# A Macaron block on one core: Y of the next batch made earlier, W of the last two batches on two engines, a clearing moved

## Chip, cores and metric

The kernel runs on 1 core of one Trainium2 chip. The metric is the device time of one execution in microseconds (us), lower is better. The core has five engines that run side by side and meet at semaphores: TensorE (PE), VectorE (DVE), ScalarE (ACT), GpSimd (POOL) and SyncE (SP, which issues DMAs here).

## The reference, cut to what matters

The block is FFN, attention, FFN over x of shape (8, 512, 256) in float32, each with a layer norm ahead and a residual behind. The FFNs have a shared expert and 8 routed ones, one per token. The diff's main part is in the attention:

```
k, q, v = split_heads(x @ Wk), split_heads(x @ Wq) / 4, split_heads(x @ Wv)   # 16 heads of 16
q_l, k_l = means over 8 neighbours -> 64 landmarks per head
s1 = softmax(q @ k_l.T)      # 512 x 64
s2 = softmax(q_l @ k_l.T)    # 64 x 64
s3 = softmax(q_l @ k.T)      # 64 x 512
z = s2.T / (max column sum * max row sum)
for _ in range(6):
    xz = s2 @ z
    z = 0.25 * z @ (13 I - xz @ (15 I - xz @ (7 I - xz)))
out = s1 @ (z @ (s3 @ v))    # then out @ Wo + bo
```

## The kernel before

The program has three parts: the first FFN (`ffn_*(0)`), the attention (`attention_*`) and the second FFN (`ffn_*(1)`). Each engine has its own hand-written list of instructions. An engine works through its list in order; a wait holds everything behind it on that engine.

**Attention.** The 8 batches (512 tokens, `GW`) go through a pipeline by periods, `for b in PERIODS` (-3 to 7). In period `b` the iterations for the inverse of batch `b` run, as the one serial chain, and all other work is put between its steps: for `nxt = b + 1` the maxima and exponentials of s3, s2 and s1, `T = s3 v`, and the start of its chain; for `far = b + 2` the transposes and projections to q and k; for `old = b - 1` the sums over heads and the denominators; for `done = b - 2` the output projection.

The inverse is not formed. The chain keeps, for each of 8 head pairs, X = [Y | T-part], 64 + 16 columns (`XC`, one buffer for even and one for odd batches). Y starts as s2.T s2, scaled (`start_y`: 32 small products on TensorE, L1909, into two of the banks 2 to 5; the scaling on DVE, L865). T's part starts as a product with s2 (`start_t`, L1954, copied by ACT, L1234, `product_kept`). One iteration `it` (0 to 5) is:

- POOL makes W = Y - I, in two halves of 4 pairs (`chain_w`, L1490); there is one buffer W;
- TensorE's **first product** W X (`chain_first`, L1933);
- ACT makes BU from it (`chain_b`, L1197), DVE makes ST (`chain_s`, L885), each in two halves, where the first half of the one is ahead of the second half of the other;
- TensorE's **second product** (`chain_second`, L1946);
- DVE updates X in two halves (`chain_x`, L896).

Around it, by name and line: `s3_max` (TensorE L1840, DVE L798, 4 reads of 128x1024) and `s1_max` (L1875 and L805, 4 reads, "quarters") make the products whose row maxima DVE takes; all of them, `s2_scores` (L1848), the exponentials' products, Y's products and the spread denominators (L1975) share banks 2 to 5 (`grid`). `landmarks` (L778) sums q and k, `query_block` (L783) lays q_l out by blocks; ACT rounds that to `QBDR` (L1315). `turn_nm1` (L1857) transposes the maxima of s1, ACT keeps them (L1312). `heads` (L1961), `denominators` (L1967, reciprocal on DVE L905), `heads_norm` (DVE L911) serve batch `old`. `project_qk` (L1823), four groups of 6 matmuls per batch, and `column_sums` (L1913; its maximum is DVE's `column_max`, L842, then `pair_scale`, L849) share bank 6; the row sums go `turn_rows`, `row_max`, `spread_rows` (L1903), `row_kept` (L837). `project` (L1580) is the output projection, `project_v` (L1833) that of v. `low_outputs` (POOL L1512) makes the low parts that `project` needs.

At the end of period `b` before the change, DVE took all four quarters of the s1 maxima before T's scaling, X's last update and Y's scaling; TensorE waited for these maxima before Y's products; POOL made the first W after Y's scaling, and the next first product waited for that W.

**Routed tiles.** In the FFN the tokens are gathered in 39 tiles (13 x 3). TensorE multiplies a tile with the expert's gate and up weights (`through`, L1735), each split in a high part (ACT L1115) and a low part (DVE L679, `low_weights`). `RY` holds three tiles of results; DVE clears it once (L703), and POOL's first gathers of residuals into it wait for that (`ry_clear`).

## Time and profile before

| what | value |
|---|---|
| median of 3 runs (lowest, highest) | 1156.12 us (1154.26, 1157.37) |
| the profiled execution's own time | 1155.66 us |
| its span | 1153.8 us |
| mean granted TensorE clock | 0.979 |
| busy: PE, DVE, ACT, POOL | 94%, 66%, 51%, 49% |
| share of the chain that ended last: PE, DVE, ACT | 83%, 9%, 3% |

Read it so: the span is the profiled part of one execution, and 1.9 us of its time lie around it. Busy shares are of the whole span; the attention lies between about 400 and 778 us of it. The chain that ended last is the row of work that set the end, followed back from the last instruction. A granted clock of 1.00 is 2.4 GHz, 0.50 is 1.2 GHz.

### The profile page before, as it was taken

How to read it: one execution, taken by the hardware profiler on the slowest of the kernel's cores; microseconds unless marked ns; L12 is line 12 of the kernel's file. 1: busy time of each engine (PE TensorE's matmuls, PEld its weight loads, DVE VectorE, ACT ScalarE, POOL GpSimd, SP SyncE). 2: the span in 40 equal slices, each digit the busy share in tenths (PEclk: the TensorE clock that was granted, in tenths of full speed). 3: DMA queues.
4: the chain of work that ended last, by engine and by line, in shares of the span. 5: the costliest groups of instructions: out<-in, count | busy, mean ns of one | idle time of the engine just before them, and what ended most of it. 6: DMA issues, size and time to landing. Idle time of an engine off the chain costs nothing.

```text
span 1153.8 us, 30074 instructions
## 1 busy us (share of the span) xinstructions
PE 1088.2 (94%) x11278; PEld 878.9 (76%) x11279; DVE 758.1 (66%) x1401; ACT 584.3 (51%) x961; POOL 565.5 (49%) x774
## 2 busy tenths in 40 slices
PE   8999999999999678899999998779999999999997
PEld 6788888888888557677667677558888888888886
DVE  6736746676767557778878867655346566767674
ACT  4334336666665445465465564344443256566663
POOL 5720734667675624345435442336301726666664
PEclk9999999999999887999999999889999999999999
DMA  7272144222211210000000000004241242212220
GB/s 255 74 306 96 37 147 143 61 73 68 68 60 38 92 56 2 3 3 3 3 3 3 3 3 3 20 21 182 92 183 37 73 161 69 64 62 61 73 64 14
DMA packets 39472, 80.25 MB, mean 70 GB/s; under 512 B 6452, under 2 KB 31159, under 8 KB 38336
## 3 DMA queue, kind: packets, MB, share of 16 engines
q1 hardware_dynamic: 27568, 52.94, 12.8%
q0 software_dynamic: 11232, 25.20, 7.1%
q8 instruction: 81, 1.33, 0.5%
q10 hardware_dynamic: 560, 0.52, 0.1%
q14 instruction: 31, 0.25, 0.1%
HBM read 57.13 MB, written 27.00 MB: 73 GB/s over the span
## 4 chain that ended last, share of the span: by engine, by line
PE 83%; DVE 9%; ACT 3%; issue 2%; POOL 2%; DMA 1%; ACTq 0%; DVEq 0%; POOLq 0%
PE PS L1735 19%; PE PS L1649 12%; PE PS L1749 12%; PE PS L1665 7%; PE PS L1823 3%; DVE A_NM L805 3%; PE PS L1742 3%; PE PS L1933 3%; PE PS L1946 2%; PE PS L1833 2%; PE PS L1580 2%; PE PS L1683 2%; PE PS L1961 1%; PE PS L1893 1%; PE PS L1867 1%
## 5 line engine op out<-in xcount | busy, mean ns | idle before, releaser
L1735 PE MATMUL PS<-WHL,XGH 128*128 128x512 f32 x624 | 217.4, 429 | 2.1 <-DVE WHL L679 2.1
L1749 PE MATMUL PS<-WD,XNT 128*128 x624 | 149.7, 383 | 1.5 <-ACT XNT L1129 1.5
L1490 POOL TENSOR_TENSOR A_W<-A_XC,CB 128x256 f32<-128x256 f32 x96 | 69.8, 748 | 153.0 <-DVE A_XC L896 131.4
L700 DVE SCALAR_TENSOR_TENSOR XNT<-PS,SCORES,XNT 128x512 f32<-128x512 f32 x78 | 58.6, 751 | 120.5 <-PE PS L1735 109.9
L1398 POOL DMA_INDIRECT X<-xs_dram,WHO x78 | 103.2, 1323 | 57.6 <-issue 23.1
L1124 ACT ACTIVATE XNT<-PS,SCORES 128x512 f32<-128x512 f32 x78 | 53.8, 689 | 145.7 <-PE PS L1735 143.7
L1735 PEld LDWEIGHTS PS<-WHL,XGH 128*128 128x128 f32 x624 | 111.4, 189 | 20.4 <-DVE WHL L679 2.6
L1749 PEld LDWEIGHTS PS<-WD,XNT 128*128 128x128 f32 x624 | 112.6, 190 | 16.0 <-issue 2.2
L1735 PE MATMUL PS<-WHL,XGL 128*128 128x512 f32 x312 | 123.2, 395 | 0.0
L1392 POOL TENSOR_SCALAR XNT<-WD 128x128 f32<-128x128 f32 x64 | 52.5, 840 | 128.7 <-DVE WD L573 128.7
L1665 PE MATMUL PS<-SDH,HHL 128*128 128x256 f32 x512 | 103.9, 287 | 1.7 <-DVE X L613 1.3
L630 DVE TENSOR_TENSOR HHL<-HSB,HHL 128x512 fp32r<-128x512 f32 x64 | 45.8, 715 | 82.0 <-ACT HHL L1089 82.0
L1404 POOL DMA_INDIRECT HSB<-shared_dram,WHO x78 | 80.5, 1032 | 38.7 <-issue 18.9
L679 DVE TENSOR_TENSOR WHL<-WG,WHL 128x1024 fp32r<-128x1024 f32 x78 | 94.8, 1216 | 3.3 <-ACT WHL L1115 3.3
L1089 ACT CAST HHL<-HSB 128x512 fp32r<-128x512 f32 x64 | 39.7, 620 | 112.7 <-PE PS L1665 76.1
L679 DVE TENSOR_TENSOR WHL<-WU,WHL 128x1024 fp32r<-128x1024 f32 x78 | 95.5, 1224 | 0.0
L1665 PEld LDWEIGHTS PS<-SDH,HHL 128*128 128x128 f32 x512 | 82.8, 188 | 10.4 <-issue 9.2
L1115 ACT CAST WHL<-WG 128x1024 fp32r x78 | 82.5, 1058 | 1.7 <-issue 1.7
L1115 ACT CAST WHL<-WU 128x1024 fp32r x78 | 82.5, 1057 | 0.0
L1649 PE MATMUL PS<-XHL,SGH 128*128 128x512 f32 x256 | 80.8, 397 | 1.5 <-DVE XHL L460 1.5
L1649 PE MATMUL PS<-XHL,SUH 128*128 128x512 f32 x256 | 81.1, 399 | 0.0
L1083 ACT ACTIVATE HSB<-PS 128x512 f32<-128x512 f32 x64 | 38.3, 599 | 79.1 <-PE PS L1649 78.9
(273 smaller groups left out, 2527.0 us busy)
## 6 DMA issues: line engine op xcount, KB each, us to landing
xs_dram<-WG SPq DMA_DIRECT2D x16, 512.0 KB, 3.0
WU<-in_r_up SPq DMA_DIRECT2D x2, 4096.0 KB, 15.1
shared_dram<-X SPq DMA_DIRECT2D x16, 512.0 KB, 2.9
WG<-in_r_gate SPq DMA_DIRECT2D x2, 4096.0 KB, 17.1
WD<-in_r_down SPq DMA_DIRECT2D x4, 2048.0 KB
X<-in_x SPq DMA_DIRECT2D x7, 512.0 KB, 9.1
X<-mid_dram SPq DMA_DIRECT2D x7, 512.0 KB, 3.9
X<-xs_dram,WHO POOLq DMA_INDIRECT x78
```

The lines of the kernel that those rows point to most:

```text
L679: dve.tensor_tensor(WHL[2 * slot + 1][:], B[w][:, bass.ds(ex * (KD * F), KD * F)], WHL[2 * slot][:].bitcast(F32), ALU.subtract).then_inc(s ...
L700: dve.scalar_tensor_tensor(B["RH"][:, u * F:(u + 1) * F], banks[3 + u][:], score(t), B["RS"][:, u * F:(u + 1) * F], ALU.mult, ALU.mult).th ...
L1115: act.copy(WHL[2 * slot][:], B[w][:, bass.ds(ex * (KD * F), KD * F)]).then_inc(s["whi"], 1)
L1124: act.activation(B["RS"][:, u * F:(u + 1) * F], banks[1 + u % 2][:], ACT.Silu, scale=B["SCORES"][:, bass.ds(t, 1)]).then_inc(s["rsilu"], 1)
L1392: hot = pool.tensor_scalar(B["ROW_HOT"][t], B["ROW_NO"], B["SROWF"][:, t:t + 1], None, ALU.is_equal)
L1398: pool.indirect_dma_start(out=B["XS"][:, u * D:(u + 1) * D], out_offset=None, in_=xs_dram, in_offset=bass.IndirectOffsetOnAxis(ap=B["WHO"] ...
L1404: pool.indirect_dma_start(out=B["RY"][:, u * D:(u + 1) * D], out_offset=None, in_=shared_dram, in_offset=bass.IndirectOffsetOnAxis(ap=B["W ...
L1490: pool.tensor_tensor(B["W"][:].rearrange("p (a m) -> p a m", m=M)[:, part, :], B["XC"][b % 2][:].rearrange("p (a w) -> p a w", w=XW)[:, pa ...
L1649: ins = pe.matmul(banks[bank][:], w[:, part], tok[:, k * GW:(k + 1) * GW], start=at == 0, stop=at == len(steps) - 1)
L1665: ins = pe.matmul(to, h[:, j * P:(j + 1) * P], w[:, part], start=(f == 0 and i == 0 and j % 2 == 0), stop=(f == KF - 1 and i == 2), skip_g ...
L1735: ins = pe.matmul(banks[bank][:], tok, w[:, k * F:(k + 1) * F], start=(k == 0 and i == 0), stop=(k == KD - 1 and i == 2))
L1749: ins = pe.matmul(banks[7][:, 0:D], B["HT"][:, u * F + f * P:u * F + (f + 1) * P], B["WD"][:, bass.ds(ex * (KF * D) + f * D, D)], start=(f ...
```

## The change

Nothing is computed otherwise; instructions change their place, and some their engine.

- **Y of `nxt`** (TensorE): `column_sums` moves from behind iteration 4's second product to right behind its first product, `project_qk(far, 2)` behind that and behind a new wait for the column maximum (`cs`). `start_y` moves from behind iteration 5's second product to right behind iteration 4's, with a wait for `heads_norm(old)`; `pv` and `s1_max(nxt, 0)` follow, the latter with a new wait for Y's scaling. `s1_max(nxt, 1)` goes behind iteration 5's second product.
- **DVE**: `column_max` and `pair_scale` ahead of `heads_norm`; Y's scaling behind X's update of iteration 4; the s1 maxima one quarter ahead of iteration 5's ST, one behind it, and the other two behind X's last update. The key landmarks go from the end of the period to behind iteration 0's ST; s3 maxima are taken one quarter ahead of X's update of iteration 0 and the other three behind.
- **Next period's opening** (TensorE): `turn_nm1` behind iteration 0's first product, then `denominators`, `s3_max(nxt, 0)`, `heads(old, 1)`; `s3_max(nxt, 1)` behind the transposes of `far`. ACT's two copies for them move likewise.
- **POOL**: the first W of `nxt` ahead of `weights_scaled`, with a wait for batch b's last first product (one buffer W).
- **W of batches 6 and 7** (`W_ON_BOTH`), iterations 1 to 5: POOL makes the half of pairs 4 to 7, DVE the other right behind X's update.
- **Clearing**: the memset of `RY` goes behind the low parts of tile 2's tokens and tile 1's up weights.

```diff
+    W_ON_BOTH = (NG - 2, NG - 1)
...
-                if first:
-                    dve.memset(B["RY"][:], 0.0).then_inc(s["ry_clear"], 1)
                 if ahead >= 2:
                     low_tile(t + 2, (u + 2) % UNR)
                 if ahead >= 1:
                     low_weights("WU", ex[u + 1], 2 * t + 3, (2 * u) % 3)
+                if first:
+                    dve.memset(B["RY"][:], 0.0).then_inc(s["ry_clear"], 1)
...
# DVE, chain_x
+                if b in W_ON_BOTH and it < PINV_ITERS - 1:
+                    dve.wait_ge(att["x"], count("x", b, 2 * it + 2))
+                    less_one(b)
+
+            def less_one(b):
+                dve.tensor_tensor(pairs(B["W"][:])[:, 0:PC, :], chain(b)[:, 0:PC, 0:M], const("eye2").unsqueeze(1).broadcast_to([P, PC, M]),
+                                  ALU.subtract).then_inc(att["w"], 1)
...
# DVE, the periods
                 if exists(nxt):
-                    s3_max(nxt, 0)
+                    landmarks(nxt, 1, 0)
+                    landmarks(nxt, 1, 1)
                 if exists(old):
                     denominators(old)
+                if exists(nxt):
+                    s3_max(nxt, 0, (0,))
                 chain_x(b, 0)
                 if exists(nxt):
-                    s3_max(nxt, 1)
+                    s3_max(nxt, 0, (1,))
+                    s3_max(nxt, 1, (0, 1))
...
                 if exists(nxt):
                     row_kept(nxt)
+                    column_max(nxt)
+                    pair_scale(nxt)
                 if exists(old):
                     heads_norm(old)
                 chain_x(b, 4)
                 if exists(nxt):
-                    s1_max(nxt, 0, (0, 1))
+                    start_y(nxt)
+                    s1_max(nxt, 0, (0,))
                 chain_s(b, 5)
+                if exists(nxt):
+                    s1_max(nxt, 0, (1,))
                 if b == NG - 1:
                     denominators(b)
-                if exists(nxt):
-                    column_max(nxt)
-                    s1_max(nxt, 1, (0,))
-                    pair_scale(nxt)
-                    s1_max(nxt, 1, (1,))
...
                 chain_x(b, 5)
                 if exists(nxt):
-                    start_y(nxt)
+                    s1_max(nxt, 1, (0, 1))
                 if exists(far):
                     landmarks(far, 0, 1)
                     query_block(far)
-                    landmarks(far, 1, 0)
-                    landmarks(far, 1, 1)
...
# ACT: both copies go from the period's end to behind chain_b(b, 0)
+                    act.copy(B["QBDR"][:], B["QBD"][:]).then_inc(att["bdr"], 1)
...
+                    act.copy(B["NM1T"][:], banks[7][:]).then_inc(att["nm1"], 1)
...
# POOL
-                for n, c in enumerate((1, 0)):
+                for n, c in enumerate((1,) if b in W_ON_BOTH and it else (1, 0)):
...
+                            wait_alone(att["c1_ready"], count("c1_ready", b - 1, PINV_ITERS))
...
+                chain_w(nxt, 0)
                 if exists(b):
                     weights_scaled(b)
-                chain_w(nxt, 0)
...
# TensorE, the period's opening
                 chain_first(b, 0)
+                if exists(b):
+                    pe.wait_ge(att["s1m"], count("s1m", b, 4))
+                    pe.wait_ge(att["qk"], count("qk", nxt, 4))
+                    turn_nm1(b)
+                if exists(old):
...
+                    denominators(old)
                 if exists(nxt):
...
+                    pe.wait_ge(att["s1m"], count("s1m", b, 4))
                     s3_max(nxt, 0)
...
                 chain_second(b, 0)
-                if exists(nxt):
+                if nxt == 0:
...
                     s3_max(nxt, 1)
...
+                if exists(nxt) and nxt > 0:
+                    pe.wait_ge(att["qkr"], count("qkr", nxt, 4))
+                    pe.wait_ge(att["s3m"], count("s3m", nxt, 2))
+                    s3_max(nxt, 1)
 
                 chain_first(b, 1)
...
# TensorE, iterations 4 and 5
                 chain_first(b, 4)
-                if exists(far):
-                    if far > 0:
-                        pe.wait_ge(att["qk"], count("qk", far, 2))
-                    project_qk(far, 2)
-                if exists(nxt):
+                if exists(nxt):
+                    pe.wait_ge(att["qk"], count("qk", far, 2))
+                    pe.wait_ge(att["tts"], count("tts", nxt, 1))
+                    column_sums(nxt)
                     pe.wait_ge(att["rmax"], count("rmax", nxt, 2))
                     spread_rows(nxt)
...
                     spread_denominators(old)
+                if exists(far):
+                    if far > 0:
+                        pe.wait_ge(att["qk"], count("qk", far, 2))
+                    pe.wait_ge(att["cs"], count("cs", nxt, 1))
+                    project_qk(far, 2)
 
                 chain_second(b, 4)
                 if exists(nxt):
+                    pe.wait_ge(att["ot"], count("ot", old, 2))
                     pe.wait_ge(att["e3"], count("e3", nxt, 4))
+                    pe.wait_ge(att["e1"], count("e1", b, 4))
+                    start_y(nxt)
                     pe.wait_ge(att["rs"], count("rs", nxt, 1))
                     pv(nxt, 1)
...
+                    pe.wait_ge(att["y0"], count("y0", nxt, 2))
...
                     s1_max(nxt, 0)
...
                     project_qk(far, 3)
+                if exists(nxt):
...
                     turn_sums(nxt)
...
+                chain_second(b, 5)
+                if exists(nxt):
+                    pe.wait_ge(att["s1m"], count("s1m", nxt, 2))
+                    s1_max(nxt, 1)
                     pe.wait_ge(att["tm"], count("tm", nxt, 1))
                     pe.wait_ge(att["x"], count("x", b, 2 * PINV_ITERS))
                     start_t(nxt)
```

## Rows read from the trace of the kernel before

**Rows 1.** The page: its first line.

```profile
span 1153.8 us, 30074 instructions
```

**Rows 2.** Busy time by stretch: us, then each engine, PEclk, DMA share, GB/s.

```profile
610.70:654.30 43.60, 41.48 (x918) 31.64 (x918) 35.58 (x81) 24.10 (x47) 20.32 (x36) 1.00 0.01 3
...
736.20:743.00 6.80, 6.80 (x88) 4.77 (x92) 1.30 (x5) 1.09 (x4) 2.04 (x3) 0.50 0.01 2
```

**Rows 3.** Timeline of TensorE, period 4 into 5: start us, us, instruction [idle before <-releaser].

```profile
638.40 0.78 PE L1933 MATMUL PS<-A_XC,A_W 64*64 64x80 f32 x32
...
640.70 0.27 PE L1903 MATMUL PS<-CB,A_RMAX 8*128 8x8 f32 x1
...
641.56 0.78 PE L1946 MATMUL PS<-A_BU,A_ST 64*64 64x80 f32 x32
...
645.10 0.78 PE L1933 MATMUL PS<-A_XC,A_W 64*64 64x80 f32 x32
...
650.40 1.15 PE L1909 MATMUL PS<-A_S 64*64 64x64 f32 x32 [0.68 <-DVE A_NM L805]
...
654.29 0.78 PE L1933 MATMUL PS<-A_XC,A_W 64*64 64x80 f32 x32 [0.27 <-issue]
...
663.28 0.78 PE L1946 MATMUL PS<-A_BU,A_ST 64*64 64x80 f32 x32 [0.19 <-ACT A_BU L1197]
```

**Rows 4.** Timeline of VectorE, period 4 into 5.

```profile
640.64 0.42 DVE L885 SCALAR_TENSOR_TENSOR A_ST<-PS,CB 128x256 f32<-128x256 f32 x1 [0.96 <-ACT A_BU L1197]
641.12 0.17 DVE L837 COPY A_SM<-PS 128x8 f32<-128x8 f32 x1
...
644.02 2.36 DVE L805 TENSOR_REDUCE A_NM<-PS 128x16 f32<-128x1024 f32 x2 [0.23 <-PE PS L1875]
...
646.96 0.68 DVE L842 TENSOR_REDUCE A_SM<-PS 128x8 f32<-128x512 f32 x1
...
650.61 0.34 DVE L896 SCALAR_TENSOR_TENSOR A_XC<-A_XC,PS 128x64 f32<-128x64 f32 x2
651.65 0.76 DVE L865 TENSOR_TENSOR A_XC<-PS,A_SM 128x256 f32<-128x256 f32 x2 [0.70 <-PE PS L1909]
...
653.03 0.56 DVE L783 TENSOR_TENSOR A_QBD<-A_QL,CB 128x256 f32<-128x256 f32 x1
...
655.13 0.90 DVE L885 SCALAR_TENSOR_TENSOR A_ST<-PS,CB 128x256 f32<-128x256 f32 x2 [0.34 <-PE PS L1933]
655.94 2.35 DVE L798 TENSOR_REDUCE A_NM<-PS 128x2 f32<-128x1024 f32 x2
...
662.25 0.89 DVE L885 SCALAR_TENSOR_TENSOR A_ST<-PS,CB 128x256 f32<-128x256 f32 x2
```

**Rows 5.** Timeline of TensorE: period 0's start, periods 6 and 7, second routed tile.

```profile
435.64 1.30 PE L1933 MATMUL PS<-A_XC,A_W 64*64 64x80 f32 x32 [1.27 <-POOL A_W L1490]
...
724.55 0.78 PE L1933 MATMUL PS<-A_XC,A_W 64*64 64x80 f32 x32
...
736.19 1.97 PE L1909 MATMUL PS<-A_S 64*64 64x64 f32 x32 [2.19 <-DVE A_NM L805]
...
742.63 0.91 PE L1933 MATMUL PS<-A_XC,A_W 64*64 64x80 f32 x32
...
754.26 1.35 PE L1933 MATMUL PS<-A_XC,A_W 64*64 64x80 f32 x32 [2.24 <-POOL A_W L1490]
...
774.18 0.36 PE L1580 MATMUL PS<-A_WOH,A_OTH 128*128 128x256 f32 x1 [0.16 <-POOL A_OTL L1512]
...
946.24 0.73 PE L1735 MATMUL PS<-WHL,XGH 128*128 128x512 f32 x2 [1.05 <-DVE WHL L679]
```

**Rows 6.** Timeline of GpSimd in period 7.

```profile
752.75 1.41 POOL L1490 TENSOR_TENSOR A_W<-A_XC,CB 128x256 f32<-128x256 f32 x2 [1.33 <-DVE A_XC L896]
```

**Rows 7.** Timeline of VectorE: period 6, and the first routed tile.

```profile
709.72 0.42 DVE L783 TENSOR_TENSOR X<-A_KL,CB 128x256 f32<-128x256 f32 x1
...
944.08 0.70 DVE L703 MEMSET HSB<- 128x768 f32 x1
```

More of the change, by code:

```diff
@@ L1296, in attention_scalar @@
                 if exists(far):
+                    rounded(far, 1)
                     projected(far, 2)
-                    rounded(far, 1)
                     rounded(far, 2)
@@ L1310, in attention_scalar @@
                     product_kept(nxt)
-                    act.wait_ge(att["nm1_ready"], count("nm1_ready", nxt, 1))
-                    act.copy(B["NM1T"][:], banks[7][:]).then_inc(att["nm1"], 1)
-                if exists(far):
-                    act.wait_ge(att["qbd"], count("qbd", far, 1))
-                    act.copy(B["QBDR"][:], B["QBD"][:]).then_inc(att["bdr"], 1)
             first_high(1)
```

39 lines of the change are left out of this document (15 added, 24 removed).

## The prediction

> **What bounds the kernel now.** I read the page first (a span of 1153.8 us [rows 1]), then the timelines of one steady period of the attention part. The chain that ended last runs mostly on TensorE (PE; its share stands in the table above), so the diff has to act through TensorE's order of work. Outside the attention part it touches only the clearing of rows. In the attention part one period takes 43.6 us, and TensorE is busy for 41.5 of them [rows 2]. What is left to win in a full period is therefore about 2.1 us. It sits in a few holes: 0.68 us in front of the Y products, where TensorE waits for the last row maxima, 0.27 us in front of the next period's first product, and small ones around the maxima [rows 3]. VectorE (DVE) is the second engine to watch: from its last update of X in a period (650.61) to the ST of iteration 1 in the next (662.25) it idles only 0.70 us ahead of Y's scaling and 0.34 us ahead of the first ST, 1.04 us of 11.64 [rows 4]. The ends of those two chains meet: DVE makes the ST at 662.25, as soon as the s3 maxima are done, and TensorE starts iteration 1's second product on it at 663.28 [rows 3, 4].
>
> **The change part by part.** I walk period 4 to 5, with its own times. A start follows a predecessor's start by a little less than its busy time, since instructions overlap by 0.05 to 0.1 us; a hand-over costs 0.06 to 0.14 us.
>
> *Iteration 4 and 5, Y moved up.* The projection of the far batch (L1823, 1.59 us: from 638.40 + 0.71 to the spread of row maxima at 640.70) was ahead of the second product [rows 3]. It now waits until the column maximum is read, because both use one bank. ST's second half starts at 640.64 and takes 0.42, the kept row maximum 0.17, the column maximum 0.68 (as at 646.96) [rows 4]: done at 641.9. The projection then runs to 643.54, and iteration 4's second product starts there, not at 641.56: 2.0 us late [rows 3]. TensorE waits 0.8 us in it. Behind it: X's update to 645.3, Y products (1.15) beside it, Y's scaling on DVE (0.76) to 646.2 [rows 3, 4], then the first s1 maxima's product, which now waits for that scaling, and iteration 5's first product at 646.96 instead of 645.10. From the first maxima (644.02) to X (650.61) DVE's list took 6.6 us before [rows 4]; two of its four quarters of maxima (2.3) and the column maximum with its two small followers (0.9) are gone from it, so X comes 3.4 us after 647.09, at 650.45 against 650.61. So DVE is where it was. But Y and W now are made (W by GpSimd, POOL, behind the low parts, at about 650.7, not needed before 652.7), and the 0.68 and 0.27 us holes close: T's product at 650.95, its copy, the heads, and the next first product at 652.72 instead of 654.29: 1.57 us won.
>
> *Next period, up to iteration 1.* DVE's stretch of 11.64 us loses the idle 1.04 and Y's scaling (0.68 to the next start), and gains two quarters of the maxima (2.27 us without overlap). Key landmarks only change place in it. That is 12.2 us. New waits: 0.2 us for the late s1 product, and 0.6 us because the second s3 product may write its banks only when DVE has read the first four, and is now behind the transposes (DVE idle from 660.4 to about 661.1). Total 13.0: ST of iteration 1 starts at 663.4 instead of 662.25 [rows 4], and the second product at 664.4 instead of 663.28 [rows 3]. **1.15 us lost per full period**; TensorE has an empty stretch from 661.8 to 663.55, waiting for the maxima of s3 (that wait was short before). The moved transposes of NM1, the denominators and heads keep TensorE at most 0.9 us longer before its second product (about 4.6 us after the first, 3.9 before); DVE is later than that and covers it. The ACT copies moved (0.4 and 0.6 us) are covered likewise, by the denominators. From iteration 1's second product on TensorE was full up to the next iteration 4 [rows 2], so the loss is carried. Periods 1 to 5: 5 x 1.15 = +5.8 us. Lower bound: nothing lost (0), upper: DVE and TensorE waits add, 2 us each (+10).
>
> *Period 6.* The same 1.15 and DVE's half of W in front of the s3 maxima, 0.42 us by the like operation alone, 0.56 beside POOL [rows 4, 7], about 0.5: +1.7 (0.5 to 2.5).
>
> *Period 6 to 7.* Before, 724.55 to 742.63 is 18.1 us, with a 2.19 us hole ahead of Y's products, after which the granted clock was 0.50 (1.2 GHz) and Y's products took 1.97 us for 1.15 [rows 2, 3, 5]. By the same walk without a far batch: second product as before, heads' scaling now behind the column maximum, so Y products at +5.3, iteration 5's first product at +8.0, the next first product at +13.9. That is 4.2 us less at the full clock. Two holes of 1.8 and 1.0 us remain there; the clock had also fallen in front of 435.64, where a product took 1.30 us for 0.78 behind a hole of 1.27 [rows 5]. So I take the fall as still there and give its price back, by the same steps in both states: 742.63 - 736.19 = 6.4 us against 654.29 - 650.40 = 3.9 us, 2.5 us [rows 3, 5]. Term: -1.7 (-4.2 to 0).
>
> *Period 7, W on two engines.* POOL's pair takes 1.41 us [rows 6]; TensorE waited 2.24 us for it at 754.26 [rows 5]. With DVE's half, W ends 0.5 us sooner in the three iterations where it came last; 0.2 more at iteration 1; and POOL, one operation (0.7 us) shorter in the last iteration, frees the low outputs that released 774.18 [rows 5]. Sum -1.9. Edges: -1 and -3. Where POOL ran, a DVE product of two SBUF operands took 0.56 us, 0.42 where it did not [rows 4, 7]: a mutual slowing of a third. The Trainium skill, SBUF — State Buffer, "Who interferes with whom", calls the shared port pair an exclusive lock and says that a DVE instruction with two SBUF inputs contends with a GpSimd instruction that reads SBUF. By a full lock DVE's half would start only behind POOL's, and win 0.2 instead of 0.5 us each time, some 1 us less in all, so +3.2 for the whole sum below. The rows show a slowing and no lock, and I keep to them.
>
> *Start.* Period 0's first product waited 1.27 us for W at 435.64 [rows 5]; that goes, but the clock is low there, and the DVE stretch then holds it as above: -0.5 (-1.5 to +1).
>
> *Clearing.* The memset (0.70 us, 0.62 to the next start) stood ahead of the low weights that TensorE waited 1.05 us for [rows 5, 7]. It goes behind them, in front of weights that TensorE needs only a tile later; POOL's gather of residuals, which waits for the memset too, had waited for a store instead. Both FFNs: -1.2 (-1.3 to 0).
>
> Sum: +5.8 + 1.7 - 1.7 - 1.9 - 0.5 - 1.2 = +2.2 us. The profiled execution took 1155.66 us (the span and 1.9 around it), 0.5 under the median of 1156.12. **Forecast 1158 us.** About 0.3%, 3.5 us, is what a measurement of this kernel can tell from no change.
>
> **Rivals.**
> *The clock falls in the new hole (slower).* In each of periods 1 to 6 TensorE would stand still for some 1.75 us in front of the s2 scores, with small tiles on both sides. It fell behind holes of 1.27 and 2.19 us [rows 5]. If it falls there, V's projections and what follows run at 1.2 GHz; one fall costs 2.5 us as above. It decides from the first fall on (1160.5). Two to four falls: 1163 to 1168. Against it: the full periods kept a granted clock of 1.00 through their holes of up to 0.68 us [rows 2, 3], the stretches where it fell were emptier around the hole, too, and 1.75 us lies between the two lengths.
> *The DVE stretch is no bound (faster).* If the s1 maxima slip into DVE's idle time, or the walk is long by 1.2 us, periods 1 to 6 lose nothing (then +0.5 for period 6's half of W), the last boundary may keep the full clock (-4.2), and the sum is -0.5 + 0.5 - 4.2 - 1.9 - 1.2 = -7.3: 1148 us; 1151 with the fall. For it: TensorE's order has 1.6 us fewer holes at each boundary. Against: DVE was idle only 1.04 of 11.64 us there [rows 4], and 1.6 us of work is moved in.
> *Y isn't ahead.* It now waits for the heads' scaling to have read its banks; if that is late in full periods too, as I have it in period 6, 1 us more per period: 1164.
>
> **How the numbers follow.** Forecast case 0.36, clock rival 0.31, DVE rival 0.27, late Y 0.06. Faster by over 0.3%: 0.27; within: 0.36; slower: 0.37. The likeliest case alone spans 1154 to 1161 by the bounds of its terms. The range reaches into both large rivals, 1148 to 1168, and leaves out the far end of each and of late Y.
>
> **What would show it.** In the profile after: iteration 4's second product 5.1 us behind its first product (3.2 before); Y's products right behind it; first product of iteration 0 about 14.3 us after that of iteration 4 (15.9 before); ST of iteration 1 right behind the second s3 maxima, with TensorE idle up to 1.8 us in front of L1848; full periods of 44.7 us instead of 43.6; the granted clock in V's projections 1.00, or 0.50 if the first rival is right. Wrong if full periods are 43 us or shorter, or if the memset is no longer followed by 0.4 us of waiting in place of 1.05 at the second routed tile.

## The result and the profile after

The changed kernel takes 1163.13 us (median of 5 runs, 1162.35 to 1165.60), the kernel before beside it 1154.61 us (median of 5, 1154.11 to 1157.37). The ratio is 1.0072, 95% interval 1.0055 to 1.0089: slower by 0.7%. The profiled execution is the one of 1163.13 us.

The page's first line, and two windows (columns as in [rows 2]), the first of them period 4 to 5:

```profile
span 1161.3 us, 30087 instructions
```

```profile
612.95:657.36 44.41, 41.55 (x920) 31.58 (x917) 35.37 (x81) 24.04 (x46) 20.07 (x36) 1.00 0.01 3
534.20:537.40 3.20, 3.17 (x41) 3.03 (x42) 1.99 (x5) 0.59 (x1) 1.10 (x2) 0.50 0.00 0
```

The full period grew from 43.60 us [rows 2] to 44.41 with the same TensorE work in it (41.48 and 41.55 us busy). The second window is new in kind: a stretch inside the full periods at the lower clock (0.50, 1.2 GHz). Before, the clock was full from 480 to 736 us.

TensorE's timeline of the same period. First product 4 starts at 643.03, so 4.63 us are to be taken off to lay it over [rows 3]:

```profile
643.03 0.78 PE L1945 MATMUL PS<-A_XC,A_W 64*64 64x80 f32 x32
643.75 1.12 PE L1925 MATMUL PS<-A_S,CB 128*128 128x512 f32 x2
...
648.08 0.78 PE L1958 MATMUL PS<-A_BU,A_ST 64*64 64x80 f32 x32
648.68 1.10 PE L1921 MATMUL PS<-A_S 64*64 64x64 f32 x32
...
651.39 0.78 PE L1945 MATMUL PS<-A_XC,A_W 64*64 64x80 f32 x32
...
657.36 0.78 PE L1945 MATMUL PS<-A_XC,A_W 64*64 64x80 f32 x32
...
664.95 0.51 PE L1852 MATMUL PS<-A_KTR,A_QBDR 32*128 32x512 f32 x4
...
668.01 0.67 PE L1860 MATMUL PS<-A_KLS,A_QBD 32*128 32x64 f32 x16 [1.84 <-DVE A_NM L799]
```

Second product 4 stands 5.05 us behind first product 4 (3.16 before), Y (L1921) right behind it, and the next period's first product 14.33 us behind first product 4 (15.89 before). Up to there 1.56 us are won. Then TensorE waits 1.84 us for the third softmax's maxima ahead of the second softmax's scores (L1860; "the scores' wait" below). VectorE's timeline shows why:

```profile
654.88 0.34 DVE L897 SCALAR_TENSOR_TENSOR A_XC<-A_XC,PS 128x64 f32<-128x64 f32 x2
...
658.71 0.75 DVE L886 SCALAR_TENSOR_TENSOR A_ST<-PS,CB 128x256 f32<-128x256 f32 x2
659.38 1.27 DVE L779 TENSOR_REDUCE A_KL<-A_KT 128x64 f32<-128x512 f32 x2
...
665.50 2.36 DVE L799 TENSOR_REDUCE A_NM<-PS 128x2 f32<-128x1024 f32 x2 [0.65 <-PE PS L1852]
667.78 0.75 DVE L886 SCALAR_TENSOR_TENSOR A_ST<-PS,CB 128x256 f32<-128x256 f32 x2
```

From X's last update (654.88) to ST of iteration 1 (667.78) it is 12.90 us (11.64 before [rows 4]); from ST(0) to ST(1) 9.07 us, where it was 662.25 - 655.13 = 7.12. The two key reductions (1.27) and an empty 0.65 us stand in it.

To see where the whole 8 us come from, the starts of all 96 chain products (8 batches, 6 iterations, 2 products each) were laid beside those of before. How far each kernel is behind the kernel before, in us, in one profiled execution each (e1 to e12 are the experiments below; "first 2, 6" is iteration 2's first product in period 6):

| product (start before) | changed | e2 | e3 | e4 | e5 | e6 | e8 | e11 |
|---|---|---|---|---|---|---|---|---|
| second 1, 0 (444.68) | -0.10 | +1.66 | +3.52 | +3.64 | +2.25 | +2.73 | +1.99 | +3.22 |
| second 1, 1 (488.50) | +1.24 | +3.07 | +4.99 | +5.30 | +3.06 | +3.65 | +1.90 | +3.73 |
| second 1, 2 (530.85) | +3.38 | +5.26 | +5.92 | +9.15 | +5.36 | +5.97 | +1.91 | +6.06 |
| second 1, 4 (619.72) | +4.63 | +6.37 | +6.34 | +12.04 | +10.17 | +4.85 | +1.57 | +7.39 |
| second 1, 5 (663.28) | +5.48 | +7.20 | +7.19 | +15.18 | +10.88 | +5.12 | +1.56 | +8.37 |
| first 2, 6 (710.62) | +9.35 | +10.71 | +8.91 | +22.20 | +17.84 | +7.27 | +2.34 | +9.45 |
| first 0, 7 (742.63) | +6.55 | +10.27 | +6.95 | +21.52 | +15.07 | +5.21 | +2.60 | +9.44 |
| second 5, 7 (773.37) | +8.14 | +11.42 | +10.47 | +22.36 | +18.20 | +6.10 | +4.81 | +11.49 |

Differences of a row between two kernels carry the start of the attention with them (the first row), which moved by up to 3 us between executions: only the growth from row to row is read. Between 4 and 5, without a fall of the clock, the changed kernel loses 0.85 us; this is called the steady loss below. The two periods before it, without a fall too, lose a little less: 0.67 us from first product 2 of period 2 to that of 3, and 0.72 from 3 to 4 (the 1.36 us told of below added). From first product 2 of period 0 to that of period 6, six periods on, it lost 11.0 us and not 6 x 0.85: one clock fall in each of periods 1, 2 and 6 (granted clock 0.50 from 486.3, 534.1 and 711.6 us on) goes with 2.0, 1.2 and 2.2 us beyond the steady loss. An empty 1.3 us of the kernel before at 599 us did not come back (1.36 us given back, between the third and the fourth line of the table, so that the loss is 9.35 + 0.32 + 1.36 = 11.0 us from first product 2 of period 0 at -0.32). The lower clock is not a matter of one execution: its mean over the span was 0.969 to 0.975 in the five executions of the changed kernel, and 0.977 to 0.986 in those of the kernel before that were timed beside the experiments.

Where the three falls begin differs. That of period 2 comes 0.6 us behind the scores' wait (its scores start at 533.47). That of period 1 comes ahead of it, 0.7 us behind another wait of 1.53 us (485.61, L1852). That of period 6 begins some 0.3 us into the scores' wait (its scores start at 713.19), and an empty 1.30 us ahead of L1852 (710.14) stands just before.

Periods 6 and 7 and the clearing, TensorE, after:

```profile
179.59 0.73 PE L1747 MATMUL PS<-WHL,XGH 128*128 128x512 f32 x2 [0.33 <-DVE WHL L680]
...
192.90 0.44 PE L1695 MATMUL PS<-CB,X 128*128 128x128 f32 x2 [1.25 <-DMA X<-xs_dram,WHO]
...
739.06 1.97 PE L1921 MATMUL PS<-A_S 64*64 64x64 f32 x32 [1.57 <-DVE A_OT L919]
...
749.18 0.78 PE L1945 MATMUL PS<-A_XC,A_W 64*64 64x80 f32 x32
...
775.54 0.78 PE L1958 MATMUL PS<-A_BU,A_ST 64*64 64x80 f32 x32 [1.20 <-ACT A_BU L1207]
```

### The profile page after: what moved, and what is told of

Its sections match the earlier page's. It is cut to its first block, busy times and chain, and to the rows that moved or that the text cites. A ratio compares the mean times of both kernels' runs of the same rounds, so it can differ in the third digit from the quotient of the medians.

```text
span 1161.3 us, 30087 instructions
## 1 busy us (share of the span) xinstructions
PE 1089.2 (94%) x11278; PEld 882.5 (76%) x11279; DVE 764.2 (66%) x1411; ACT 584.3 (50%) x961; POOL 556.1 (48%) x764
## 4 chain that ended last, share of the span: by engine, by line
PE 83%; DVE 8%; ACT 3%; issue 2%; DMA 2%; POOL 1%; ACTq 0%; DVEq 0%; POOLq 0%; SPq 0%
PE PS L1747 18%; PE PS L1661 12%; PE PS L1761 11%; PE PS L1677 7%; PE PS L1835 4%; PE PS L1958 3%; PE PS L1754 3%; PE PS L1845 2%; PE PS L1592 2%; PE PS L1945 2%; DVE A_NM L799 2%; PE PS L1695 2%; PE PS L1905 1%; PE PS L1979 1%; PE PS L1973 1%
## 5 line engine op out<-in xcount | busy, mean ns | idle before, releaser
L1502 POOL TENSOR_TENSOR A_W<-A_XC,CB 128x256 f32<-128x256 f32 x86 | 61.6, 735 | 188.4 <-DVE A_XC L897 178.1
L1409 POOL DMA_INDIRECT X<-xs_dram,WHO x78 | 100.2, 1285 | 57.6 <-issue 23.1
```

The lines of the kernel that those rows point to most:

```text
L1409: pool.indirect_dma_start(out=B["XS"][:, u * D:(u + 1) * D], out_offset=None, in_=xs_dram, in_offset=bass.IndirectOffsetOnAxis(ap=B["WHO"] ...
L1502: pool.tensor_tensor(B["W"][:].rearrange("p (a m) -> p a m", m=M)[:, part, :], B["XC"][b % 2][:].rearrange("p (a w) -> p a w", w=XW)[:, pa ...
```

## The experiments

Three theories. **Sum**: VectorE's longer stretch loses 0.85 us in each full period. **Clock**: the wait it leaves on TensorE makes the clock fall, and that is the larger part. **Split**: W on two engines costs instead of giving. Each kernel was timed beside the kernel before on the same chip, ratios with 95% intervals.

**e11, the key reductions alone** (on the kernel before).

```
@@ vector engine, end of the period
                     query_block(far)
-                    landmarks(far, 1, 0)
-                    landmarks(far, 1, 1)
@@ behind ST(0)
+                if exists(nxt):
+                    landmarks(nxt, 1, 0)
+                    landmarks(nxt, 1, 1)
                 if exists(nxt):
                     s3_max(nxt, 0)
```

> The kernel before with one part of the change alone: the two reductions of the key landmarks (1.27 us) moved from the end of a period on VectorE behind ST(0) of the next. Theory 'VectorE's stretch from ST(0) to ST(1) bounds second product 1': it comes 1.0 to 1.3 us later behind second product 0 in each full period, TensorE waits some 1.5 us before the second softmax's scores (0.2 us before), and the clock falls behind that wait in some of the periods: the sum over seven periods 5 to 8 us plus 1 to 2.3 us a fall, ratio 1.005 to 1.012. Rival 'ST(0) starts 1.27 us sooner when the reductions leave its way, so that the stretch only begins earlier': ST(0) in the kernel before waited for first product 0, and not for the reductions (they ended 0.34 us before it), so this would need at least that wait: a time within 2 us of the kernel before.

Measured: 1163.62 us, ratio 1.0072 (1.0059 to 1.0085), as much as the whole change. VectorE in its period 4 to 5:

```profile
662.50 0.90 DVE L885 SCALAR_TENSOR_TENSOR A_ST<-PS,CB 128x256 f32<-128x256 f32 x2 [1.53 <-PE PS L1934]
663.32 1.27 DVE L778 TENSOR_REDUCE A_KL<-A_KT 128x64 f32<-128x512 f32 x2
...
670.63 0.88 DVE L885 SCALAR_TENSOR_TENSOR A_ST<-PS,CB 128x256 f32<-128x256 f32 x2
```

ST(0) to ST(1) is 8.13 us, 1.01 more than before, and the table's last column grows by 0.98 us from period 4 to 5. Where the reductions stood they had been free: here VectorE waits 1.53 us for first product 0 in their place (0.34 before [rows 4]). The loss is as the sum theory has it; the place of the wait is not: it stands now ahead of first product 1, and TensorE's wait for the scores stayed short (1.9 us in seven periods). One fall of the clock came, in period 1, and the two around 745 and 762 us were longer than the two of before (10.2 us, 6.8 before); period 7 lost 2.05 us. The clock is no large part of this kernel's loss, though: two of its executions had a mean clock of 0.979 and took 1163.43 and 1164.32 us, while the five of the kernel before beside it with that same mean clock took 1155.0 to 1156.8 us.

**e4, the same reductions put back, in the changed kernel** (the edit of e11 reversed).

> The changed kernel with the two reductions of the key landmarks (0.65 us each) put back from VectorE's stretch behind ST(0) to the end of the period before, where they stood. Theory 'VectorE's stretch from ST(0) to ST(1) sets second product 1': TensorE's wait before the second softmax's scores shrinks from 1.84 to about 0.6 us, second product 1 comes 1.3 us sooner behind second product 0, and the time is 4 to 7 us under the changed kernel's (six periods by 0.6 to 1.2 us), 1156 to 1159 us, with fewer clock falls behind that wait. Rival 'VectorE's end of the period has no room': T and first product 0 of the next period, or ST(0), come 1.3 us later, and the time is within 1.5 us of the changed kernel's, 1162 to 1165 us.

Measured: 1174.72 us, ratio 1.0152 (1.0132 to 1.0172), some 11 us *slower* than the changed kernel. Neither theory had that. ScalarE of e4 (period 4) and of the changed kernel (period 5), which are 37.74 us apart when first product 0 of the one is laid over that of the other:

```profile
622.67 0.44 ACT L1206 ACTIVATE A_BU<-PS 128x320 f32<-128x320 f32 x1 [1.76 <-DVE A_ST L886]
623.00 0.40 ACT L1263 CAST A_QBDR<-A_QBD 128x256 fp32r<-128x256 f32 x1
```

```profile
659.16 0.44 ACT L1207 ACTIVATE A_BU<-PS 128x320 f32<-128x320 f32 x1 [0.52 <-DVE A_ST L886]
659.50 0.40 ACT L1264 CAST A_QBDR<-A_QBD 128x256 fp32r<-128x256 f32 x1
```

The change put `QBDR` behind BU(0) in ScalarE's list. BU's second half waits for ST(0), and ST(0) now waits for the reductions: it is 1.25 us later, `QBDR` with it, and the third softmax's first scores, all heads and second product 0 behind them 0.7 us. TensorE of e4, where the changed kernel has no wait (660.54):

```profile
623.54 0.51 PE L1851 MATMUL PS<-A_KTR,A_QBDR 32*128 32x512 f32 x4 [0.67 <-ACT A_QBDR L1263]
```

So in the new order the reductions can't go back to their old place with `QBDR` where it now is: Y ahead has filled the end of the period on VectorE. The stretch gained nothing, the scores' wait stayed (12.3 us in seven periods), and now the clock fell in five periods, in this wait or less than 2 us behind it (the mean clock was 0.965 to 0.972 in the five executions). Its column grows by 1.6 us a period without a fall (period 3 to 4, with the 1.36 us added), and by 3.9 and 3.1 with one (1 to 2, 4 to 5).

**e6, the round trip covered.** Both pairs of maxima ahead of X(0) again; on TensorE the second round of scores ahead of the turned tokens.

```
-                    s3_max(nxt, 0, (0,))
+                    s3_max(nxt, 0, (0, 1))
                 chain_x(b, 0)
                 if exists(nxt):
-                    s3_max(nxt, 0, (1,))
                     s3_max(nxt, 1, (0, 1))
... (and on TensorE, s3_max(nxt, 1) with its two waits ahead of the turned tokens of far)
```

> The changed kernel with both pairs of the first four third-softmax maxima ahead of X(0) again on VectorE, and the second round of their scores ahead of the turned tokens on TensorE. In the changed kernel VectorE runs out of work for 0.65 us before the last two pairs, because their scores can be written only when the pair just ahead is read. Theory 'that round trip and not VectorE's sum adds to the stretch up to second product 1': X(0) covers it, VectorE's wait shrinks from 0.65 to 0.2 us or less, second product 1 comes 0.4 to 0.6 us sooner behind second product 0 in each full period, and the time is 2.5 to 4 us under the changed kernel's (ratio 1.004 to 1.005). Rival 'VectorE's work alone bounds the stretch' (the forecast): X(0) 1.2 us later makes W(0) and first product 1 later by as much and nothing is won: within 1 us of the changed kernel's, or slower.

Measured: 1161.38 us, ratio 1.0045 (1.0031 to 1.0058), as expected, though the interval still touches the changed kernel's (1.0055 to 1.0089). VectorE's wait is 0.29 us (0.2 or less was expected), TensorE's before the scores 0.72 in place of 1.84.

```profile
665.14 2.36 DVE L799 TENSOR_REDUCE A_NM<-PS 128x2 f32<-128x1024 f32 x2 [0.29 <-PE PS L1851]
```

```profile
667.64 0.67 PE L1859 MATMUL PS<-A_KLS,A_QBD 32*128 32x64 f32 x16 [0.72 <-DVE A_NM L799]
```

Its column grows by 0.27 us from period 4 to 5 in place of 0.85, so that second product 1 comes 0.58 us sooner there. It still has falls in periods 1 and 6.

**e5, the third projection behind second product 4.**

```
+                chain_second(b, 4)
                 if exists(far):
                     if far > 0:
                         pe.wait_ge(att["qk"], count("qk", far, 2))
                     pe.wait_ge(att["cs"], count("cs", nxt, 1))
                     project_qk(far, 2)
-
-                chain_second(b, 4)
```

> The changed kernel with the third Q and K projection (1.64 us) put behind second product 4 instead of ahead of it. Theory 'TensorE's work between first product 4 and first product 5 is the bound, with 0.78 us of waiting for the column maxima in it': second product 4 comes 2.3 us sooner, but first product 5 only by the wait that goes, 0.5 to 0.8 us in each full period; the time is 3 to 5 us under the changed kernel's (ratio to the kernel before 1.003 to 1.0045). Rival, the forecast's reading (the delay of second product 4 runs on through X(4) to first product 5 one for one): first product 5 comes 1.9 to 2.3 us sooner in each full period and the time is 9 us or more under, faster than the kernel before. Second rival, the later projections (QT, KT, their rounding on ScalarE) become late next: within 1.5 us of the changed kernel's.

Measured: 1172.28 us, ratio 1.0136 (1.0120 to 1.0153): no theory's time, but the first one's step. Second product 4 came 2.2 us sooner and first product 5 only 0.45 us; the steady loss was 0.71 us in place of 0.85. The rest is the clock. It fell in five periods, each time in the scores' wait or less than 1 us from it (12.3 us of it in seven periods; in period 1 a wait of 1.53 us ahead of L1852 stands before it), for 1.3 to 2.3 us. Its mean clock was 0.964 to 0.967 in all four executions. Why it fell there in five periods and in the changed kernel, with the same wait, in three is open.

**e3, the scores' wait filled** with unread matmuls into a grid bank the maxima had left.

```
                 chain_first(b, 1)
+                if exists(nxt) and nxt > 0:
+                    pe.wait_ge(att["s3m"], count("s3m", nxt, 3))
+                    for _ in range(5):
+                        pe.matmul(banks[GB][:, 0:P], ident, CB[:, 0:P], start=True, stop=True)
```

> The changed kernel with five extra matmuls of 128 by 128 fp32 into a free grid bank in the wait of TensorE before the second softmax's scores, in each full period; they wait for the third pair of maxima, so some 1.1 us of the 1.84 us wait is filled and nothing that is on the path waits for them. Their results are overwritten unread. Theory 'the clock falls behind this hole' : the falls at 487, 535 and 712 us (and the one in the first product of period 6) do not come, the mean granted clock rises from 0.975 to 0.98, and the time is 3 to 5 us under the changed kernel's (1158 to 1160 us, ratio 1.003 to 1.005). Rival 'the hole and VectorE's longer stretch are the whole of it, falls come and go anyway': the time stays within 1 us of the changed kernel's (ratio 1.0065 to 1.008), the hole still ends with VectorE's maxima 1.8 us behind.

Measured: 1161.76 us, ratio 1.0049 (1.0031 to 1.0067); the interval meets the changed kernel's, so of the expected 3 to 5 us only 1.4 are in the medians, and these are not clear of the noise. The mean clock did rise as expected, to 0.976 to 0.980 in the six executions. Three of them, with 0.979 and 0.980, took 1158.5 to 1161.5 us, where the kernel before beside them took 1154.8 to 1158.3 us at these two values: at a like clock some 3 to 5 us of loss stay, which the lower clock does not explain. The scores' group in the page of lines, 440 to 730 us (busy, mean ns | idle before), of the kernel before, the changed one and e3:

```profile
L1848 PE MATMUL PS<-A_KLS,A_QBD 32*128 32x64 f32 x112 | 5.2, 301 | 1.5 <-DVE A_NM L798 1.4
```

```profile
L1860 PE MATMUL PS<-A_KLS,A_QBD 32*128 32x64 f32 x112 | 6.1, 343 | 11.9 <-DVE A_NM L799 11.9
```

```profile
L1860 PE MATMUL PS<-A_KLS,A_QBD 32*128 32x64 f32 x112 | 5.2, 303 | 0.0
```

In e3's profile the falls of periods 2 and 6 are gone (+5.92 to +8.91 us from period 2 to 6, against +3.38 to +9.35), and the steady 0.85 us are the same to 0.01. But from first product 0 of period 7 to the end it loses 3.5 us, where the changed kernel loses 1.6, a fall from 745.1 us on reaching into it; over the whole chain it is 1.3 us better than the changed kernel (from +3.52 to +10.47, against -0.10 to +8.14), as in the medians. The fall in period 1 stayed, behind another wait, which no filling met, but was half as long (3.4 us for 6.8). The wait, in e3:

```profile
488.83 0.60 PE L1852 MATMUL PS<-A_KTR,A_QBDR 32*128 32x512 f32 x4 [1.52 <-DVE A_NM L799]
```

In period 1 no output projection stands ahead of the second round of scores, so that TensorE waits there too.

**e9, e6 and a filling of two matmuls together.**

> The changed kernel with the order of e6 (both pairs ahead of X(0)) and two extra unread matmuls of 128 by 128 fp32 in what is left of the wait before the second softmax's scores. Theory 'per period sum plus clock falls': e6 left 0.1 to 0.3 us of each full period's 0.85 us, but still had two clock falls behind that wait (2.06 us and 1.39 us); with the wait filled they do not come, and the time is 2 to 3.5 us under e6's: 1157.5 to 1159.5 us, ratio 1.0017 to 1.0035. Rival 'the falls are where they are by chance': the same as e6, ratio 1.0045.

Measured: 1160.55 us, ratio 1.0052 (1.0032 to 1.0071): this meets the rival's 1.0045 and not the theory's 1.0017 to 1.0035, whose upper end it only touches. Its profile (0.8 us of waiting before the scores) has one fall up to 740 us, in period 1, and is 4.3 us behind at first product 2 of period 6. Once e6 has narrowed the wait, filling what is left gives nothing to be measured.

**e2, W on GpSimd alone, in the changed kernel** (`W_ON_BOTH = ()`).

> The changed kernel with W of the last two periods left on GpSimd alone, as before. In the changed kernel VectorE's half took 0.75 us beside GpSimd's 0.73 us, where GpSimd alone needs 1.43 to 1.5 us for both. Theory 'half and half gives little': each iteration's W ends some 0.4 us sooner with the split, but VectorE's own list (statistics, ST, denominators) is 0.5 to 0.75 us later each time, so without the split the time is within 1.5 us of the changed kernel's on either side (ratio to the kernel before 1.006 to 1.0085). Rival, the forecast's own term (split worth 1.9 us in period 7 and 0.5 us cost in period 6): 1.5 us longer than the changed kernel, ratio 1.0085. Rival, the split itself costs the 1.6 us that period 7 lost: 2 us or more shorter than the changed kernel, ratio under 1.0055.

Measured: 1166.91 us, ratio 1.0103 (1.0082 to 1.0123), 3.8 us over the changed kernel in the medians; the forecast's own term (1.0085) is nearest and lies in the interval, which meets the changed kernel's. But in the profiles period 7, from its first product 0 to the end, costs the changed kernel 1.59 us and e2 1.15, all of e2's before second product 0; from there on the changed kernel loses 1.13 us and e2 nothing. What e2 lost more than the changed kernel it lost between first product 2 of period 6 and first product 0 of period 7, 2.4 us: there the clock falls of the two lie at other places, and e2 has an empty stretch of 1.47 us on TensorE with no releaser shown, which the changed kernel has not:

```profile
744.04 0.31 PE L1905 MATMUL PS<-XNT 128*32 128x64 f32 x5 [1.47 <-issue]
```

**e8, the split alone, on the kernel before.**

> The kernel before with only W of periods 6 and 7 on two engines. The changed kernel without it took 3.6 us more than with it. Theory 'the split is worth 1.5 to 3.5 us by itself': W of an iteration done some 0.7 us sooner (0.75 us beside each other instead of 1.43 us), ratio 0.997 to 0.9987. Rival 'it is given back': VectorE's half stands ahead of ST and of the third softmax's maxima in period 6, 0.8 us are lost at first product 1 there, and 1.4 us at second product 4 of period 7: within 1 us of the kernel before or slower.

Measured: 1157.43 us, ratio 1.0021 (1.0010 to 1.0032), slower by 0.2%. VectorE's half in period 6, and the scores behind it:

```profile
705.13 0.78 DVE L900 TENSOR_TENSOR A_W<-A_XC,CB 128x256 f32<-128x256 f32 x1
```

```profile
708.32 0.67 PE L1853 MATMUL PS<-A_KLS,A_QBD 32*128 32x64 f32 x16 [1.50 <-DVE A_NM L799]
```

It pushes the maxima back: +1.16 us at second product 1 of period 6. In period 7 it gives 0.4 us at first products 2 and 4 and loses 1.25 us at second product 0, 1.4 at second product 4 and 0.8 at first product 5.

**e7, the new order between periods 6 and 7 alone**, on the kernel before, without split and clearing (the changed lines of the second half of the period under `if nxt == NG - 1`, those of the first under `if b == NG - 1`).

> The kernel before with the new order of Y, column maxima, first softmax's maxima and NM1 only at the boundary between periods 6 and 7, where no Q and K projections stand between; W on GpSimd alone, the clearing as before. Theory 'the order pays only there': in the changed kernel this boundary took 15.3 us from first product 4 to the next first product 0 instead of 18.1 us, so the time is 1.5 to 3 us under the kernel before, ratio 0.9974 to 0.9987. Rival, that the 2.8 us came from W on two engines in period 6 or from where the clock happened to fall (the changed kernel without the split had 4 us less of it): within 1 us of the kernel before.

Measured: 1155.71 us, ratio 1.0001 (0.9988 to 1.0014). First product 0 of period 7 came 1.05 us sooner (-0.61 to -1.66 us in the table's terms), but second product 0 only 0.03: ST(0) then stands behind the maxima that were moved to the end. The rival's number came.

**e1, the clearing alone.**

> The kernel before with one part of the change alone: the clearing of the rows in the first feed-forward stage moved behind the two weight splits. The part theory (each part gives what its own wait in the trace gives): TensorE's waits for VectorE's low weights (2.1 us in all before, 0.6 us in the changed kernel) shrink by 1.2 to 1.5 us, and the time is 1.0 to 1.5 us under the kernel before, ratio 0.9987 to 0.9991. Rival, that the feed-forward stage is held by something else at its end and the wait only moves: within 0.3 us of the kernel before.

Measured: 1155.11 us, ratio 0.9997 (0.9988 to 1.0006). TensorE:

```profile
180.45 0.73 PE L1735 MATMUL PS<-WHL,XGH 128*128 128x512 f32 x2 [0.32 <-DVE WHL L679]
...
193.71 0.44 PE L1683 MATMUL PS<-CB,X 128*128 128x128 f32 x2 [1.24 <-DMA X<-xs_dram,WHO]
```

The wait of 1.05 us is 0.32, in both FFNs; but 13 us later in the first one TensorE waits 1.24 us for a DMA, which the kernel before didn't. e2, e5 and e12 have the short wait without this one, so it is not sure to come. What is left is too small for the runs.

**e10, the two waits around the last boundary filled, on the kernel before.**

```
... (end of the period)
                     turn_sums(nxt)
+                    if nxt == NG - 1:
+                        for _ in range(7):
+                            pe.matmul(banks[7][:, 0:P], ident, CB[:, 0:P], start=True, stop=True)
                     pe.wait_ge(att["s1m"], count("s1m", nxt, 4))
                     start_y(nxt)
@@ ahead of chain_first(b, 2)
+                if b == NG - 1:
+                    pe.wait_ge(att["y0"], count("y0", b, 2))
+                    for _ in range(5):
+                        pe.matmul(banks[GB][:, 0:P], ident, CB[:, 0:P], start=True, stop=True)
```

> The kernel before with extra unread matmuls of 128 by 128 fp32 (0.26 us each): seven in the 2.19 us wait ahead of the Y products between periods 6 and 7, five in the 2.24 us wait ahead of first product 2 of period 7. Theory 'the falls at 736.9 and 754.0 us follow those waits': both do not come, Y and T products, NM1 and the heads run at full clock (some 3.5 us of them by the rows at either level), and the time is 2.5 to 4.5 us under the kernel before, ratio 0.996 to 0.998, which would beat both kernels. Rival 'TensorE has too little to do there with or without them': the falls come 1 to 7 us later, the products after them lengthen instead, within 1 us of the kernel before.

Measured: 1152.03 us (median of 8), ratio 0.9973 (0.9962 to 0.9983): **it beats both kernels.** Y's products at the full clock, and a next first product 3.70 us behind them in place of 742.63 - 736.19 = 6.44 [rows 5]; the fall there does not come:

```profile
736.73 1.15 PE L1909 MATMUL PS<-A_S 64*64 64x64 f32 x32 [0.62 <-DVE A_NM L805]
737.68 1.09 PE L1954 MATMUL PS<-A_TM,A_S 64*64 64x16 f32 x32
738.70 0.66 PE L1857 MATMUL PS<-CB,A_NM 128*128 128x128 f32 x4
...
740.43 0.78 PE L1933 MATMUL PS<-A_XC,A_W 64*64 64x80 f32 x32
```

Of the two falls that were expected to go, the second still comes, half as long (granted clock 0.50 from 754.5 us for 3.4 us, where it was 6.8 before). In the profile 2.7 us are won up to first product 0 of period 7, 1.05 behind it.

**e12, the like filling in the changed kernel**, five matmuls behind second product 4 of period 6 and five ahead of first product 2 of period 7.

> The changed kernel with extra unread matmuls of 128 by 128 fp32 (0.26 us each): five in the 1.57 us wait ahead of the Y products between periods 6 and 7, five in the 1.83 us wait ahead of first product 2 of period 7. The same filling made the kernel before 3.1 us shorter (0.9973). Theory 'the falls at 740, 760 and 777 us follow from those waits and add to the change's cost of the full periods': the clock of this stretch stays up, and the time is 2.5 to 4 us under the changed kernel's, 1159 to 1161 us, ratio 1.0035 to 1.005, the seven full periods unchanged. Rival 'Y ahead has already covered what the filling gives': within 1 us of the changed kernel, ratio 1.0065 to 1.008.

Measured: 1162.70 us, ratio 1.0076 (1.0057 to 1.0095): nothing to be measured. Y's products run at the full clock (1.15 us), but the fall comes 8 us later (746.6 us), behind the next wait of 1.00 us, and is twice as long (6.8 us for 3.4), onto T's product (1.11 us at the full clock), the heads and first product 0:

```profile
746.55 1.84 PE L1966 MATMUL PS<-A_TM,A_S 64*64 64x16 f32 x32
```

The new order has two holes here, of 1.57 and 1.00 us, where the old one has its one of 2.19 [rows 5], and the filling met only the first. No other fall came in period 7, where the changed kernel has two (759.4 and 776.5 us), and that period lost nothing (+7.55 to +7.23 us, against +6.55 to +8.14). So the profile shows some 1.5 us won over the whole chain, which the six executions, from 1161.8 to 1167.7 us, do not bear out.

## Why the prediction was right and wrong

The time, 1163.13 us, lies in the range; the forecast of 1158 was 5 us low, and the case that came is the first rival, the clock falls in the new hole, which I gave 0.31 ("two to four falls: 1163 to 1168"; there were three). That the number lies in the rival's bracket, at its lower end, is in part luck: full periods and falls each cost less than priced, period 7 cost 1.6 us where I had it give 1.9, and 1.36 us came back that no part of the change aimed at.

- **Full periods, +1.15 us each.** Right in mechanism, a third too large: second product 4 at +5.05 us (5.1 forecast), first product 0 at +14.33 (14.3), the stretch of VectorE 12.90 us (13.0), TensorE's hole 1.84 us (up to 1.8), the period 44.41 us (44.7), and 0.85 us lost (0.67 and 0.72 in the two periods before). The 0.3 us too much are made of steps that each came 0.1 to 0.2 us sooner than I had them. e11 shows one cause I had not singled out: "key landmarks only change place in it" is true for the sum of VectorE's stretch, but their old place was covered by the wait for first product 0, and in the kernel before the move alone costs 1.01 us a period. How much of the changed kernel's loss is theirs is not shown: e4, which takes them back there, delays `QBDR` by them. e6 shows the second, the 0.65 us round trip, at its forecast size.
- **The clock in the full periods.** This step failed: I let 1.75 us of waiting pass because the clock had held through holes of 0.68 us, and called the stretches where it fell "emptier around the hole". The kernel before had more to say than the rows I read: between 480 and 736 us it held through longer holes too (1.26 us at 486.61, 1.32 at 599.96, 1.39 at 714.85), the longest of them this one:

```profile
723.05 0.51 PE L1882 MATMUL PS<-A_NM1T,A_PICK 32*128 32x512 f32 x4 [1.45 <-ACT XNT L1210]
```

  It fell in 3 of 7 periods of the changed kernel and in 5 of 7 of e4 and e5, in a stretch where TensorE is busy for 236.7 of 260 us (480 to 740 us of the changed kernel). Each cost 1.2 to 2.2 us, not 2.5. Summed, that is 5.4 us of the profiled 11 us lost up to period 6. That the scores' wait brings the falls on is shown only in part: in e3 those of periods 2 and 6 are gone with it, but the medians moved by 1.4 us with intervals that meet, and the fall of period 1 stands behind another new wait, of 1.53 us.
- **Period 6, the half of W, 0.5 us.** 0.85 us at first product 1, beyond the steady loss; e8 has 1.16 at second product 1. The half took 0.76 to 0.78 us, not 0.56.
- **Period 6 to 7, -1.7 us.** The changed kernel's profile has -2.8 from first product 2 of period 6 on, with a fall that lasted half as long as before (3.4 us for 6.8). e7 finds nothing that stays for the order alone, so this gain can't be put down to it: the term has its sign in the one profile and is not borne out by e7.
- **Period 7, -1.9 us.** Wrong sign in the profile: +1.6. W does come 0.4 us sooner at first products 2 and 4, but VectorE's half, 0.75 us beside GpSimd's 0.72, now stands ahead of its statistics and the root's constants, ST of iteration 4 starts only behind them, and second product 4 waits 1.20 us for BU (775.54) where it waited 0.20 (768.38 in the kernel before). GpSimd's half, VectorE's half and statistics, and ST:

```profile
770.92 0.73 POOL L1502 TENSOR_TENSOR A_W<-A_XC,CB 128x256 f32<-128x256 f32 x1 [5.32 <-DVE A_XC L897]
```

```profile
771.18 0.76 DVE L903 TENSOR_TENSOR A_W<-A_XC,CB 128x256 f32<-128x256 f32 x1
771.86 1.39 DVE L427 BATCH_NORM_STATS2 STATS<-X 128x6 f32<-128x256 f32 x4
...
774.55 0.75 DVE L886 SCALAR_TENSOR_TENSOR A_ST<-PS,CB 128x256 f32<-128x256 f32 x2
```

  e2, with W on GpSimd alone, loses nothing from second product 0 of period 7 on, so the split is behind these 1.13 us. I had priced the half where W was late and not what queues behind it. The Trainium skill, SBUF — State Buffer, "Who interferes with whom", has the port pair as an exclusive lock; the rows lie between its rule and mine: GpSimd's half is as long as alone, VectorE's goes from 0.42 to 0.76 us, where a full wait for the other's end (771.65) would give 0.89. Whether the split is worth its place in the changed kernel is open: e2's median says 3.8 us for it with intervals that meet, e8 0.2% against, and the profiles of both differ in where the clock fell.
- **Start, -0.5 us.** -0.3 us at first product 2 of period 0 in the one profile; executions differ there by more. First product 0 came 2.88 us sooner (432.76), but by second product 1 all but 0.1 us of it was gone.
- **Clearing, -1.2 us.** The waits shrank as forecast (0.32 us for 1.05), twice; e1 shows that the time doesn't follow, -0.3 us with an interval of 1 us to either side.

What would have shown the forecast wrong, a full period of 43 us or shorter, did not come; what would have shown the rival right, the clock of 0.50 behind the hole, did, in part of the periods.

## What to carry to other kernels

Before an operation is moved on an engine that is nearly full, look at what it stands beside: one that fills a wait is free there and can cost most of its length elsewhere. In the kernel before, two reductions of 1.27 us cost 1.01 us a period that way, in all as much as the whole change. Such costs don't simply add up, though: put back in the new order, the same two reductions made it slower still (e4), because what they then held up had moved too. A sum of waits won is not enough when a new wait of a microsecond or two is left on TensorE: price the clock falls behind it as a likely case. And filling such a wait with a few unread matmuls is worth trying before any reordering; here, with twelve of them at two places of the kernel before, it gave the only gain clear of the noise, and the like filling in the changed kernel gave none (e12).

## What the runs showed that was not expected

- In a stretch where TensorE was busy for 236.7 of 260 us, the clock fell behind a single wait of 1.84 us (period 2 of the changed kernel) and, in e6, behind two of 1.19 and 0.90 us (fall at 490.5 us); it held through the same 1.84 us in periods 3 to 5 of the changed kernel.
- Filling a wait removed the fall behind it at the first of e10's two places and, in e3's profile, in periods 2 and 6; where a second wait stood close behind, the fall came there (e12).
- A VectorE and a GpSimd operation with two SBUF inputs each, beside each other, cost a third of a microsecond in sum, and which of them pays differs. With GpSimd's half of W started 0.25 us ahead, VectorE's takes 0.75 to 0.78 us for 0.42, and GpSimd's stays at 0.72 to 0.74. At the end of a full period of the kernel before both pay: `query_block` takes 0.56 us for 0.42 [rows 4, 7], and GpSimd's pair 1.60 us for the 1.41 of [rows 6]:

```profile
652.59 1.60 POOL L1490 TENSOR_TENSOR A_W<-A_XC,CB 128x256 f32<-128x256 f32 x2 [0.84 <-DVE A_XC L865]
```

- An empty 1.3 us on TensorE at 599 us, with no releaser shown, is in the kernel before and gone in the changed one, 1.36 us that no edit aimed at; the profiles with less changed (e1, e7, e8, e10, e11) lack 0.55 us of it at the same place. Such stretches stand elsewhere in e2 (1.47 us at 744.04) and e5 (1.48 us at 611.25). Their cause is open.
